# Cross-attention and expert-choice FFN on one core: the attention's counts, reciprocals, score tails and second statistics in other places

## The chip, the cores and the metric

The kernel runs on one core of one Trainium2 chip. Its engines are TensorE (PE, with its weight loads PEld), VectorE (DVE), ScalarE (ACT), GpSimd (POOL) and SyncE (SP), which here only starts transfers. The metric is the device time in microseconds (us) of one execution; the profile's span lies inside it.

## The reference

```python
x = x + xattn(layernorm(x), ctx)          # x: (2, 2048, 512); ctx: (2, 77, 384); 8 heads of 64
    # softmax(q k^T / 8) v, then @ Wo + bo
x = x + ffn(layernorm(x))                 # 8 experts, hidden 2048
    # probs = softmax(x @ gate_w.T); each expert takes its top k tokens of a sequence
    # out[token] += gate * (gelu(x_token @ w1) @ w2)
```

All of it is in float32. The kernel builds float32 products from fp32r parts: high by high, high by low, low by high (hence three matmuls wherever one product stands).

## The kernel before

**Stages.** Setup folds Wq and Wk into A (one matrix per batch, 8 folds) and Wv and Wo into B (10 folds), so that attention is scores = XN A, softmax, out = P B. The gate's eight columns ride along in both (SC, OC). The gate columns of B come from 24 small matmuls (`pe_gate_fold`, L1036) and go back into `wo_sb` and `bo_row` on DVE (L990 to L994) before the B folds. Then comes attention: 16 blocks of two tiles of 128 tokens (NBLK = 16, TPB = 2), in steps i = -1 to 16, in a pipeline over several blocks. Then come the experts: the chosen rows are gathered and run through up, Gelu and down.

**One attention step i.** Every engine has its own fixed order (`step` in `pe_attention`, `act_attention`, `dve_attention`, `pool_attention`, `sp_attention`); semaphores join them. PE: transposes of the probabilities of block i-1 (L1095; the last 104 columns of each tile are the tails), scores of block i in two tiles of two halves (L1056 to L1058, `three`), output product of block i-1 tile 0, transposes of the normalised block i+1 (`pe_xT`, L1032), output product tile 1. ACT: high parts of the transposed probabilities (`pTh`, tails first, L847, L848), eight exps per tile with the row sum (`exp`, L839), normalising of block i-2 into XN2 (L819), gate exps of block i-2 (L811), high part of the transposed block (`xTh`, L826), normalising of block i+2. DVE: `dve_x1` (x + attention and the gate logits, L911, L913), low parts (`pTl` L945, L949, `xTl` L919), the score maximum as a minimum of the negated scores (L931), statistics by bn_stats and bn_aggr of the residual X1 (block i-2) and of x (block i+2) (L875, L880), reciprocals of the row sums (L925), gate (L894 to L900). POOL: small [128, 2] steps that make the reciprocal deviation (`pool_rstd2` L752, `pool_rstd1` L732), gate logit repair, and scaling of the probabilities by the reciprocals (L803). The transposes wait for that scaling.

**Counts.** Which 512 tokens an expert takes is found by a search of 15 rounds (`dve_round` L523, `pe_round` L553): DVE narrows the threshold by the last totals, makes three candidates, compares and counts per partition (L549); PE sums over partitions with a matrix of ones (L555). For batch 0 these rounds run in steps 9 to 14, up to three per step (`round_at`, slots 0, 1, 2). Slot 2 of a step is counted by PE at the start of the next one, slot 0 after the transposes, slot 1 before the last score half. Masks and places follow in steps 14 and 15 (`dve_masks`, `dve_chosen`, `dve_places`, `dve_rows`), then the rows are looked up by a one-hot product (L646, L654), and POOL gathers them (L786) at step 16.

## Time and profile before

| | |
|---|---|
| median of 3 runs | 1773.19 us (1773.03 to 1773.25) |
| profiled execution | 1772.58 us, its span 1770.9 us |
| PE busy | 1702.3 us (96%), 8702 matmuls |
| DVE, ACT, POOL busy | 1099.1, 798.9, 346.5 us |
| granted PE clock, mean | 0.979 |

How to read the rows further down. In windows: stretch, its length, busy time and instructions (x) of PE, PEld, DVE, ACT, POOL, then the granted clock of TensorE (1.00 is 2.4 GHz, 0.50 is 1.2 GHz), the DMA share and GB/s. In waits: who waited for whom, us in total, times, longest. In the timeline: start, duration, engine, line, operation, output and input, count, and in brackets the idle time ahead of it and what ended it. In groups: busy us and mean ns, then idle time. A step begins with its first transpose (L1095): 87.0 (step 2), 103.1, 120.5, 137.8, 155.4, 172.9, 190.3, 207.9, 228.5 (step 10), 251.8, 276.2, 299.5, 321.6, 340.8, 361.2.

### The profile page before, as it was taken

How to read it: one execution, taken by the hardware profiler on the slowest of the kernel's cores; microseconds unless marked ns; L12 is line 12 of the kernel's file. 1: busy time of each engine (PE TensorE's matmuls, PEld its weight loads, DVE VectorE, ACT ScalarE, POOL GpSimd, SP SyncE). 2: the span in 40 equal slices, each digit the busy share in tenths (PEclk: the TensorE clock that was granted, in tenths of full speed). 3: DMA queues.
4: the chain of work that ended last, by engine and by line, in shares of the span. 5: the costliest groups of instructions: out<-in, count | busy, mean ns of one | idle time of the engine just before them, and what ended most of it. 6: DMA issues, size and time to landing. Idle time of an engine off the chain costs nothing.

```text
span 1770.9 us, 23364 instructions
## 1 busy us (share of the span) xinstructions
PE 1702.3 (96%) x8702; PEld 1448.2 (82%) x8702; DVE 1099.1 (62%) x2020; ACT 798.9 (45%) x1852; POOL 346.5 (20%) x457
## 2 busy tenths in 40 slices
PE   7999978879999999999999999999999999999997
PEld 7898978867888888888888888888888888888886
DVE  5355566667686665775575557556766675575563
ACT  4466644452332333444454445444544454454441
POOL 2133322230010302240034005100700160022002
PEclk9899988989999999999999999999999999999999
DMA  3133323323243525251134114411511261133003
GB/s 125 58 110 117 122 96 135 127 84 122 93 119 119 167 95 143 95 143 48 48 73 117 48 48 90 124 49 48 133 58 49 71 143 48 48 72 71 24 1 48
DMA packets 76660, 156.36 MB, mean 88 GB/s; under 512 B 4453, under 2 KB 5633, under 8 KB 76553
## 3 DMA queue, kind: packets, MB, share of 16 engines
q1 hardware_dynamic: 62217, 121.38, 20.0%
q0 software_dynamic: 14336, 33.56, 9.7%
q8 instruction: 67, 1.10, 0.3%
q14 instruction: 40, 0.33, 0.1%
HBM read 121.37 MB, written 33.55 MB: 87 GB/s over the span
## 4 chain that ended last, share of the span: by engine, by line
PE 85%; DVE 6%; issue 3%; POOL 3%; ACT 2%; DMA 0%; POOLq 0%; DVEq 0%; ACTq 0%
PE ps L1868 10%; PE ps L1870 10%; PE ps L1869 10%; PE ps L1846 9%; PE ps L1848 9%; PE ps L1847 9%; PE ps L1761 3%; PE ps L1762 3%; PE ps L1763 3%; PE ps L1748 3%; PE ps L1749 3%; PE ps L1750 3%; PE ps L1056 2%; DVE st L875 2%; PE ps L1057 2%
## 5 line engine op out<-in xcount | busy, mean ns | idle before, releaser
L1868 PE MATMUL ps<-v2h,hhS 128*128 128x512 f32 x768 | 300.5, 391 | 0.0
L1870 PE MATMUL ps<-v2h,hlS 128*128 128x512 f32 x768 | 298.9, 389 | 0.0
L1869 PE MATMUL ps<-v2l,hhS 128*128 128x512 f32 x768 | 298.9, 389 | 0.0
L1846 PE MATMUL ps<-Th,Wh 128*128 128x512 f32 x672 | 261.4, 389 | 0.0
L1847 PE MATMUL ps<-Tl,Wh 128*128 128x512 f32 x672 | 261.4, 389 | 0.0
L1848 PE MATMUL ps<-Th,Wl 128*128 128x512 f32 x672 | 261.4, 389 | 0.0
L1301 POOL DMA_INDIRECT out_dram<-YS,tok_idx x48 | 80.5, 1678 | 805.5 <-DVE YS L1655 797.2
L1421 ACT ACTIVATE v2h<-w_raw 128x512 fp32r<-128x512 f32 x96 | 57.7, 625 | 308.6 <-PE ps L1870 308.6
L1655 DVE SCALAR_TENSOR_TENSOR YS<-ps,tok_gate,YS 128x512 f32<-128x512 f32 x144 | 106.6, 749 | 132.1 <-PE ps L1870 132.1
L1870 PEld LDWEIGHTS ps<-v2h,hlS 128*128 128x128 f32 x768 | 144.1, 188 | 30.2
L1869 PEld LDWEIGHTS ps<-v2l,hhS 128*128 128x128 f32 x768 | 144.2, 188 | 29.4
L1868 PEld LDWEIGHTS ps<-v2h,hhS 128*128 128x128 f32 x768 | 144.2, 188 | 29.0
L1638 DVE TENSOR_TENSOR hlS<-hfS,hhS 128x512 fp32r<-128x512 f32 x192 | 128.0, 687 | 45.0 <-ACT hfS L1440 45.0
L1439 ACT ACTIVATE hhS<-hfS 128x512 fp32r<-128x512 f32 x144 | 91.1, 632 | 129.8 <-DVE hfS L1627 61.6
L1848 PEld LDWEIGHTS ps<-Th,Wl 128*128 128x128 f32 x672 | 126.1, 188 | 26.3
L1847 PEld LDWEIGHTS ps<-Tl,Wh 128*128 128x128 f32 x672 | 126.1, 188 | 26.3
L1846 PEld LDWEIGHTS ps<-Th,Wh 128*128 128x128 f32 x672 | 126.1, 188 | 26.0
L1748 PE MATMUL ps<-eTh,w1h 128*128 128x512 f32 x256 | 102.5, 401 | 5.5 <-issue 5.5
L1761 PE MATMUL ps<-w2h,hh 128*128 128x512 f32 x256 | 103.1, 403 | 0.0
L1762 PE MATMUL ps<-w2l,hh 128*128 128x512 f32 x256 | 100.8, 394 | 0.0
L1763 PE MATMUL ps<-w2h,hl 128*128 128x512 f32 x256 | 100.7, 393 | 0.0
L1749 PE MATMUL ps<-eTl,w1h 128*128 128x512 f32 x256 | 100.7, 393 | 0.0
(236 smaller groups left out, 3517.1 us busy)
## 6 DMA issues: line engine op xcount, KB each, us to landing
w_raw<-in_L_ffn_w_dram SPq DMA_DIRECT2D x80, 1024.0 KB, 5.5
XB<-in_x_dram SPq DMA_DIRECT2D x16, 512.0 KB, 4.2
XR<-in_x_dram SPq DMA_DIRECT2D x16, 512.0 KB, 6.0
out_dram<-X SPq DMA_DIRECT2D x16, 512.0 KB, 5.0
xn_rows<-XN SPq DMA_DIRECT2D x16, 512.0 KB, 5.5
w_raw<-in_L_xattn_Wq_dram SPq DMA_DIRECT2D x1, 1024.0 KB, 8.2
wo_sb<-in_L_xattn_Wo_dram SPq DMA_DIRECT2D x2, 512.0 KB, 10.0
w_raw<-in_L_xattn_Wk_dram SPq DMA_DIRECT2D x1, 768.0 KB, 4.8
```

The source lines that it names most:

```text
L1638: nc.vector.tensor_tensor(hlS[:, b, f], hfS[:, b, f], hhS[:, b, f].bitcast(F32), ALU.subtract).then_inc(s_hid, 1)
L1748: nc.tensor.matmul(ps[:, 4 + n % 2, :], wh, th, start=(k == 0), stop=False)
L1749: nc.tensor.matmul(ps[:, 4 + n % 2, :], wh, tl, start=False, stop=False)
L1761: nc.tensor.matmul(ps[:, c, :], th, wh, start=(f == 0), stop=False)
L1762: nc.tensor.matmul(ps[:, c, :], th, wl, start=False, stop=False)
L1763: last = nc.tensor.matmul(ps[:, c, :], tl, wh, start=False, stop=(f == KF - 1))
L1846: nc.tensor.matmul(ps[:, bank, :], wh, th, start=(idx in OPENS and k == 0), stop=False, **go_on)
L1847: nc.tensor.matmul(ps[:, bank, :], wh, tl, start=False, stop=False, **go_on)
L1848: last = nc.tensor.matmul(ps[:, bank, :], wl, th, start=False, stop=(k == 1), **go_on)
L1868: nc.tensor.matmul(ps[:, bank, :], th, wh, start=(t == 0), stop=False)
L1869: nc.tensor.matmul(ps[:, bank, :], th, wl, start=False, stop=False)
L1870: last = nc.tensor.matmul(ps[:, bank, :], tl, wh, start=False, stop=(t == GF - 1))
```

## The change

- x1 is a scalar_tensor_tensor that also sums the row (`sum2`). POOL makes minus the mean from it (`pool_mean2`), ACT squares the centred row with a sum (`act_squares`, into XN2 as a scratch), POOL goes on with that variance. bn_stats and bn_aggr of X1 are gone.
- ACT: the squares stand ahead of the exps, the gate exps between the two tiles' exps, the two tiles of XN2's normalising on both sides of xTh. After step 16 the squares of the last block stand ahead of the experts.
- DVE: gate scores and gate move ahead, the second reciprocal ahead of x1 and xTl; the statistics of x are taken in two halves around the maxima; round 0 after the tails, round 1 after the first maximum, round 2 before the second reciprocal.
- PE: both tiles' scaling is waited for once, the tails are transposed first with a semaphore of their own; round 0 is counted between the score tiles, round 1 after the scores, round 2 in the middle of output tile 1. POOL scales tile 0 ahead of `pool_rstd1`.
- Step 0: the first scores start ahead of Wo's transposes, the small gate matmuls are put between the matmuls of the last score half, B folds use three pairs of banks.
- Step 15: row numbers, values and one-hot stand later on DVE.

```diff
+        def fold_bank(n):
+            return (6, 2, 4)[(n - NA) % 3]
...
-            if n >= 4:
-                pe.wait_ge(e_lo, n - 3 if kind == "A" else max(n - 1, NA))
+            if kind == "A" and n >= 4:
+                pe.wait_ge(e_lo, n - 3)
+            if kind == "B" and n >= NA + 3:
+                pe.wait_ge(e_lo, n - 2)
...
-            return BANK[1] if b == 1 else 0 if k % SLOTS == 0 else 3
+            return BANK[0] if b == 0 and k % SLOTS == 0 else BANK[1]
...
+        def pool_mean2(pool, n):
+
+            pool.wait_ge(v_x1, (n + 1) * TPB)
+            if not isinstance(n, int) or n > 0:
+                pool.wait_ge(a_sq2, n)
+            pool.tensor_tensor(nm2[:], sum2[:], minus_over_d[:], ALU.mult).then_inc(g_nm2, 1)
+
         def pool_rstd2(pool, n, u, i):
 
-            pool.wait_ge(v_mv2, n + 1)
+            pool.wait_ge(a_sq2, n + 1)
+            pool.tensor_tensor(ve2[:], ssq2[:], over_d[:], ALU.mult).then_inc(g_var2, 1)
+            pool.wait_ge(g_var2, n + 1)
+            pool.tensor_tensor(ve2[:], ve2[:], eps_c[:], ALU.add).then_inc(g_ve2, 1)
+            pool.wait_ge(g_ve2, n + 1)
             if not isinstance(n, int) or n > 0:
                 pool.wait_ge(a_gexp, n)
-            pool.tensor_tensor(nb2[:], mv2[:, :, 0], minus_c[:], ALU.mult)
-            pool.tensor_tensor(ve2[:], mv2[:, :, 1], eps_c[:], ALU.add).then_inc(g_ve2, 1)
-            pool.wait_ge(g_ve2, n + 1)
+                pool.wait_ge(a_xn2, n)
             pool.tensor_tensor(rs2[:], ve2[:], pow_c[:], ALU.pow).then_inc(g_rs2, 1)
+            pool.wait_ge(g_ring, i + 2)
+            pool.wait_ge(g_nm2, n + 1)
+            pool.tensor_tensor(gdm[:], ring[u][:, 4, TPB:2 * TPB], nm2[:], ALU.add).then_inc(g_dm, 1)
             pool.wait_ge(g_rs2, n + 1)
-            pool.tensor_tensor(nb2[:], nb2[:], rs2[:], ALU.mult).then_inc(g_nb2, 1)
-            pool.wait_ge(g_ring, i + 2)
-            pool.tensor_tensor(gdm[:], ring[u][:, 4, TPB:2 * TPB], mv2[:, :, 0], ALU.subtract).then_inc(g_dm, 1)
+            pool.tensor_tensor(nb2[:], nm2[:], rs2[:], ALU.mult).then_inc(g_nb2, 1)
...
                     pool_rstd2(pool, i - 2, u, i)
+
+                def scale(t):
+                    pool.wait_ge(v_rec, 2 * i + t + 1)
+                    over = srec[:, t * H:(t + 1) * H].unsqueeze(2).broadcast_to([P, H, J])
+                    pool.tensor_tensor(PR[:, t], PR[:, t], over, ALU.mult).then_inc(g_prob, 1)
+
+                if has(i):
+                    scale(0)
                 if has(i + 2):
                     pool_rstd1(pool, i + 2, u)
                 if has(i):
-                    for t in range(TPB):
-                        pool.wait_ge(v_rec, 2 * i + t + 1)
-                        over = srec[:, t * H:(t + 1) * H].unsqueeze(2).broadcast_to([P, H, J])
-                        pool.tensor_tensor(PR[:, t], PR[:, t], over, ALU.mult).then_inc(g_prob, 1)
+                    scale(1)
             steps(pool, step)
...
+        def act_squares(act, n, u):
+
+            act.wait_ge(g_nm2, n + 1)
+            for t in range(TPB):
+                last = nc.scalar.activation(XN2[:, u, t, :], X1[:, u, t, :], ACT.Square, bias=nm2[:, t:t + 1],
+                                            accum_out=ssq2[:, t:t + 1])
+            last.then_inc(a_sq2, 1)
...
                 if has(i - 1):
+                    act.wait_ge(p_tails, i)
+                    nc.scalar.activation(pTh[0:TAIL, :, NCH - 1, :], tails, ACT.Copy).then_inc(a_tails, 1)
                     act.wait_ge(p_pT, i)
-                    nc.scalar.activation(pTh[0:TAIL, :, NCH - 1, :], tails, ACT.Copy).then_inc(a_tails, 1)
...
+                if has(i - 2):
+                    if not isinstance(i, int) or i >= 4:
+                        act.wait_ge(d_xn2[u], 16 * half - 16)
+                    act_squares(act, i - 2, u)
...
                 if has(i):
                     exp(i, 0, u)
+                if has(i - 2):
+                    act_gate_exp(act, i - 2)
+                if has(i):
                     exp(i, 1, u)
                 if has(i - 2):
-                    if not isinstance(i, int) or i >= 4:
-                        act.wait_ge(d_xn2[u], 16 * half - 16)
-                    act_normalise(act, X1[:, u], rs2, nb2, XN2[:, u], g_nb2, a_xn2, i - 2)
-                    act_gate_exp(act, i - 2)
+                    act_normalise(act, X1[:, u], rs2, nb2, XN2[:, u], g_nb2, a_xn2, i - 2, (0,))
                 if transposed(i, has):
                     act_xTh(act, i + 1)
+                if has(i - 2):
+                    act_normalise(act, X1[:, u], rs2, nb2, XN2[:, u], g_nb2, a_xn2, i - 2, (1,))
...
+            act.wait_ge(d_xn2[(NBLK - 1) % 2], 16 * (NBLK // 2 - 1))
+            act_squares(act, NBLK - 1, (NBLK - 1) % 2)
...
-            nc.vector.tensor_tensor(X1[:, u, t].rearrange("p (h d) -> p h d", h=2), out_halves(t),
-                                    XR[:, u, t].rearrange("p (h d) -> p h d", h=2), ALU.add).then_inc(v_x1, 1)
+            nc.vector.scalar_tensor_tensor(out=X1[:, u, t].rearrange("p (h d) -> p h d", h=2), in0=out_halves(t),
+                                           scalar=1.0, in1=XR[:, u, t].rearrange("p (h d) -> p h d", h=2),
+                                           op0=ALU.mult, op1=ALU.add, accum_out=sum2[:, t:t + 1]).then_inc(v_x1, 1)
...
             def step(i, u, half, has):
...
                 if has(i - 2):
                     dve_x1(dve, i - 2, 1, u, None, None)
-                if round_at(i, 0) is not None:
-                    dve_round(dve, 0, round_at(i, 0))
                 if has(i - 1):
                     dve.wait_ge(a_tails, i)
...
+                if round_at(i, 0) is not None:
+                    dve_round(dve, 0, round_at(i, 0))
+                if has(i - 1):
                     dve.wait_ge(a_pTh, i)
...
-                if round_at(i, 1) is not None:
-                    dve_round(dve, 0, round_at(i, 1))
                 if at(i, CHOICE + 1):
                     dve_places(dve, 0, 1)
-                    dve_rows(dve, 0)
-                    dve_vals(0, 0, 1)
-                    dve_one_hot(0)
-                if has(i):
-                    maximum(i, 0)
-                if has(i - 2):
-                    if not isinstance(i, int) or i > 2:
-                        dve.wait_ge(g_dm, i - 2)
-                    dve.wait_ge(v_x1, 2 * i - 2)
-                    stats(X1[:, u], st2, v_st2)
                 if has(i + 2):
                     dve.wait_ge(d_x[u], 16 * half + 32)
                     if has(i + 1):
                         dve.wait_ge(g_sd, i + 2)
-                    if has(i - 2):
-                        dve.wait_ge(v_st2, i - 1)
-                    stats(XB[:, u], st1, v_st1)
-                elif has(i - 2):
-                    dve.wait_ge(v_st2, i - 1)
+                    nc.vector.bn_stats(st1[:, 0, :], XB[:, u, 0, :])
+                if has(i):
+                    maximum(i, 0)
+                if at(i, 0):
+                    dve.wait_ge(p_woT, 2)
+                    for c in range(2, KD):
+                        nc.vector.tensor_copy(woT[:, c, :], ps[:, 4 + c, :]).then_inc(e_woT, 1)
+                if round_at(i, 1) is not None:
+                    dve_round(dve, 0, round_at(i, 1))
                 if has(i - 2):
-                    aggregate(st2, mv2, v_mv2)
-                if has(i + 2):
-                    dve.wait_ge(v_st1, i + 3)
-                if at(i, CHOICE):
-                    dve.wait_ge(p_s, 2 * i + 2)
-                    dve_masks(dve, 0)
+                    dve_gate_scores(dve, i - 2)
+                if at(i, 0):
+                    dve.wait_ge(p_boT, 1)
+                    nc.vector.tensor_copy(boT[:], ps[:, 5, 64:64 + KD]).then_inc(e_boT, 1)
                 if has(i):
                     maximum(i, 1)
                 if has(i + 2):
+                    nc.vector.bn_stats(st1[:, 1, :], XB[:, u, 1, :]).then_inc(v_st1, 1)
+                    dve.wait_ge(v_st1, i + 3)
+                if has(i):
+                    reciprocal(i, 0)
+                if has(i + 2):
                     aggregate(st1, mv1, v_mv1)
+                if at(i, CHOICE + 1):
+                    dve_rows(dve, 0)
+                if has(i - 2):
+                    dve_gate(dve, i - 2)
+                if round_at(i, 2) is not None:
+                    dve_round(dve, 0, round_at(i, 2))
+                if at(i, CHOICE):
+                    dve_masks(dve, 0)
+                if has(i):
+                    reciprocal(i, 1)
+                if has(i - 1):
+                    dve_x1(dve, i - 1, 0, 1 - u, 16 * half + 16 * u,
+                           16 * half - 16 + 16 * u if not isinstance(i, int) or i >= 3 else None)
                 if at(i, 0):
                     dve.wait_ge(p_wog, 1)
...
-                if has(i - 2):
-                    dve_gate_scores(dve, i - 2)
-                if has(i):
-                    reciprocal(i, 0)
-                if has(i - 1):
-                    dve_x1(dve, i - 1, 0, 1 - u, 16 * half + 16 * u,
-                           16 * half - 16 + 16 * u if not isinstance(i, int) or i >= 3 else None)
                 if transposed(i, has):
                     dve_xTl(dve, i + 1)
-                if has(i - 2):
-                    dve_gate(dve, i - 2)
-                if has(i):
-                    reciprocal(i, 1)
...
-                if round_at(i, 2) is not None:
-                    dve_round(dve, 0, round_at(i, 2))
...
                 if at(i, CHOICE + 1):
+                    dve_vals(0, 0, 1)
+                    dve_one_hot(0)
                     dve_found(dve, 0, BANK[0])
...
-
+            def three(psum, pairs, terms=None):
...
+                def others():
+                    if terms:
+                        for _ in range(2):
+                            next(terms, None)
+                    nc.tensor.matmul(psum, wh, mh, start=(k == 0), stop=False)
+                    others()
+                    nc.tensor.matmul(psum, wh, ml, start=False, stop=False)
+                    others()
+                    last = nc.tensor.matmul(psum, wl, mh, start=False, stop=(k == n - 1))
+                    if k < n - 1:
+                        others()
 
...
+            def first_scores():
+
+                pe.wait_ge(e_gwl, B)
+                pe.wait_ge(d_wo, 32)
+                pe.wait_ge(d_bo, 32)
+                for t in range(TPB):
+                    for part in range(2):
+                        if t == 0:
+                            pe.wait_ge(e_lo, 5)
+                        elif part == 0:
+                            pe.wait_ge(e_lo, NA)
+                            for c in range(KD):
+                                for k in range(KD):
...
+                            pe.wait_ge(e_woT, KD)
+                        terms = pe_gate_terms() if t and part else None
+                        scores(0, t, part, terms)
...
             def step(i, u, half, has):
                 if has(i):
                     pe.wait_ge(v_xTl, i + 1)
-                if round_at(i - 1, 2) is not None:
-                    pe_round(pe, 0, round_at(i - 1, 2))
                 if has(i - 1):
                     if at(i, 1):
-                        pe.wait_ge(e_lo, len(folds))
-                    pe.wait_ge(g_prob, 2 * i - 1)
+                        pe.wait_ge(e_lo, len(folds) - 1)
+                    pe.wait_ge(g_prob, 2 * i)
                     if has(i - 2):
                         pe.wait_ge(v_lg, 2 * i - 3)
                     flat = PR[:].rearrange("p t h j -> p (t h j)")
                     for t in range(TPB):
-                        if t:
-                            pe.wait_ge(g_prob, 2 * i)
-                        for c, (c0, n) in enumerate(CH):
-                            dst = tails[:, t, :] if c == NCH - 1 else ps[:, 4 + t, c0:c0 + P]
-                            last = nc.tensor.transpose(dst, flat[:, t * HJ + c0:t * HJ + c0 + n], ident[:])
+                        c0, n = CH[-1]
+                        last = nc.tensor.transpose(tails[:, t, :], flat[:, t * HJ + c0:t * HJ + c0 + n], ident[:])
+                    last.then_inc(p_tails, 1)
+                    for t in range(TPB):
+                        for c, (c0, n) in enumerate(CH[:-1]):
+                            last = nc.tensor.transpose(ps[:, 4 + t, c0:c0 + P],
+                                                       flat[:, t * HJ + c0:t * HJ + c0 + n], ident[:])
                     last.then_inc(p_pT, 1)
-                if round_at(i, 0) is not None:
-                    pe_round(pe, 0, round_at(i, 0))
                 if at(i, 0):
...
+                    first_scores()
+                elif has(i):
                     for t in range(TPB):
                         for part in range(2):
                             if has(i - 1) and (t, part) == (0, 1):
                                 pe.wait_ge(v_tails, i)
+                            if round_at(i, 0) is not None and (t, part) == (1, 0):
+                                pe.wait_ge(v_lg, 2 * i - 2)
+                                pe_round(pe, 0, round_at(i, 0))
                             if at(i, CHOICE + 1) and (t, part) == (1, 0):
                                 pe_before(pe, 0, 1)
                             if at(i, CHOICE + 1) and (t, part) == (1, 1):
                                 pe.wait_ge(s_placed, 2)
-                            if round_at(i, 1) is not None and (t, part) == (1, 1):
-                                pe_round(pe, 0, round_at(i, 1))
...
+                            scores(i, t, part)
+                if round_at(i, 1) is not None:
+                    pe_round(pe, 0, round_at(i, 1))
                 if at(i, 0):
...
+                    pe_gate_bias(pe)
                 if has(i - 1):
+                    if at(i, 1):
+                        pe.wait_ge(e_lo, len(folds))
                     pe.wait_ge(v_pTl, i)
                     out_tile(i, 0)
...
+                    pe.wait_ge(a_exp, 2)
                     for n in range(NA, len(folds)):
                         pe_fold(pe, n)
                 if has(i - 1):
                     if has(i - 2):
                         pe.wait_ge(v_lg, 2 * i - 2)
-                    out_tile(i, 1)
-                    if at(i, CHOICE):
-                        pe.wait_ge(a_exp, 2 * i + 2)
-                        pe_before(pe, 0, 0)
+
+                    def between():
+                        if round_at(i, 2) is not None:
+                            pe.wait_ge(a_exp, 2 * i + 2)
+                            pe_round(pe, 0, round_at(i, 2))
+                        if at(i, CHOICE):
+                            pe.wait_ge(a_exp, 2 * i + 2)
+                            pe_before(pe, 0, 0)
+
+                    out_tile(i, 1, between)
```

## Rows read from the trace of the kernel before

**Rows 1.** Windows by stage: quiet step, steps 3-9, 10-14, hand-over, experts.

```profile
87.00:103.10 16.10, 16.10 (x128) 16.10 (x126) 9.34 (x22) 11.03 (x45) 4.89 (x16) 1.00 0.21 66
103.10:225.40 122.30, 114.56 (x884) 112.29 (x882) 67.47 (x169) 77.19 (x315) 41.15 (x112) 1.00 0.35 121
225.40:340.80 115.40, 94.88 (x650) 91.85 (x649) 76.88 (x221) 53.71 (x223) 28.08 (x74) 0.88 0.37 128
340.80:385.40 44.60, 30.94 (x222) 29.49 (x222) 28.88 (x80) 18.43 (x61) 14.99 (x31) 0.82 0.28 95
385.40:1770.90 1385.50, 1370.36 (x6356) 1130.94 (x6356) 877.74 (x1454) 602.24 (x1102) 239.41 (x172) 0.99 0.29 82
```

**Rows 2.** Waits of PE, 0 to 420 us.

```profile
PE ps L555 <- DVE cnt L549: 23.5, 11, 3.7
...
PE ps L1095 <- POOL PR L803: 11.7, 9, 2.8
```

**Rows 3.** Timeline, end of a steady step and start of the next.

```profile
150.87 1.56 ACT L819 ACTIVATE XN<-X,nb,rs 128x512 f32<-128x512 f32 x2
...
152.85 1.06 ACT L826 ACTIVATE xTh<-ps 128x1024 fp32r<-128x1024 f32 x1
...
155.74 0.20 DVE L925 RECIPROCAL srec<-ssum 128x8 f32<-128x8 f32 x1
...
156.02 1.22 POOL L803 TENSOR_TENSOR PR<-PR,srec 128x616 f32<-128x616 f32 x1 [3.48 <-DVE srec L925]
...
157.29 0.77 PE L1095 MATMUL ps<-ident,PR 128*128 128x128 f32 x5 [1.13 <-POOL PR L803]
```

**Rows 4.** Timeline, the first counts.

```profile
226.16 0.93 DVE L541 TENSOR_TENSOR cand<-kept,bits 128x24 uint32<-128x24 uint32 x1
...
228.42 0.17 PE L555 MATMUL ps<-cnt,ones_bf 128*128 128x24 bf16 x1 [2.89 <-DVE cnt L549]
...
229.29 0.18 DVE L541 TENSOR_TENSOR cand<-kept,bits 128x24 uint32<-128x24 uint32 x1
...
230.10 0.55 DVE L549 TENSOR_REDUCE cnt<-hit 128x24 bf16<-128x384 bf16 x1
```

**Rows 5.** Windows after small matmuls and after the count waits.

```profile
45.80:55.40 9.60, 9.60 (x24) 6.31 (x24) 2.30 (x7) 1.63 (x2) 2.61 (x3) 0.50 0.00 0
...
229.90:236.60 6.70, 5.89 (x23) 5.89 (x24) 3.92 (x11) 1.26 (x2) 0.00 (x0) 0.50 0.47 172
```

**Rows 6.** Groups of DVE and ACT, steps 3 to 9.

```profile
L875 DVE BATCH_NORM_STATS2 st<-X 128x6 f32<-128x512 f32 x14 | 8.9, 680 | 0.0
...
L911 DVE TENSOR_TENSOR X<-ps,XR 128x512 f32<-128x512 f32 x14 | 9.4, 672 | 5.7 <-PE ps L1058 5.4 <-issue 0.3
...
L949 DVE TENSOR_TENSOR pTl<-ps,pTh 128x1024 fp32r<-128x1024 f32 x7 | 8.6, 1225 | 3.4 <-ACT pTh L848 3.4
...
L931 DVE TENSOR_REDUCE nmax<-ps 128x8 f32<-128x616 f32 x14 | 11.2, 800 | 6.2 <-PE ps L1058 6.2
...
L819 ACT ACTIVATE XN<-X,nb,rs 128x512 f32<-128x512 f32 x14 | 10.9, 852 | 0.0
...
L839 ACT ACTIVATION_READ_ACCUMULATOR PR<-ps,nmax 128x1 f32 x112 | 25.0, 223 | 0.0
```

**Rows 7.** Timeline, one-hot, gathers and hand-over to the experts.

```profile
352.36 2.29 DVE L646 TENSOR_TENSOR hot<-row,col_iota 128x2048 bf16<-128x2048 f32 x1
...
365.11 1.22 POOL L786 DMA_INDIRECT XB<-xn_rows,tok_idx  x1 [0.40 <-DMA xn_rows<-XN]
...
370.13 0.24 POOL L750 TENSOR_TENSOR ring<-ring,one_c 128x16 f32<-128x16 f32 x1
...
378.21 0.63 ACT L1346 ACTIVATE w1h<-w_raw 128x512 fp32r<-128x512 f32 x1 [4.30 <-PE ps L1058]
...
383.40 1.28 ACT L1362 ACT_TABLE_LOAD   x1
...
385.46 0.76 PE L1748 MATMUL ps<-eTh,w1h 128*128 128x512 f32 x1 [5.53 <-issue]
```

116 lines of the change are left out of this document (54 added, 62 removed).

## The prediction

> **What bounds the kernel now.** I first read the windows by stage [rows 1]: attention runs to 385.4 us, the experts take the other 1385.5 us. TensorE (PE) is busy in the experts and in the quiet attention step 2 (16.10 of 16.10 us). In steps 3 to 9 it is busy 114.56 of 122.3 us, in steps 10 to 14 94.88 of 115.4 us at a mean granted clock of 0.88, in steps 15 and 16 and the hand-over 30.94 of 44.6 us. The change touches the experts in one place only, so at most what attention loses is on offer. The list of waits [rows 2] names the losers: PE waits 23.5 us in eleven pieces for the counts (L549), 11.7 us in nine pieces for the scaled probabilities (L803). One such piece in a steady step [rows 3]: ScalarE (ACT) is done with both exps at 150.87, but the second reciprocal comes at 155.74 (on VectorE, DVE, it stands behind x1, the residual split and the gate, which waits for ACT's gate exps, which stand behind the normalising of XN2). GpSimd (POOL) then scales 1.22 us and PE starts the second half of its transposes at 157.29, after 1.13 us idle. The first step with counts [rows 4]: PE asks for count 0 right after the output product, DVE has only begun it, PE gets it at 228.42 after 2.89 us; the next round needs another chain of 1.8 us (0.4 for narrowing, then 229.29 to 230.65). These two waits cost more than they last: after the pair the granted clock is 0.50, the 1.2 GHz level, for 6.7 us [rows 5], where 6.7 us of work takes about 3.3 us at 2.4 GHz. Steady steps with one idle piece of 1.1 us stay at 1.00 [rows 1].
>
> **Steady steps 3 to 9.** Set T = 0 at the first transpose of a step; PE's own work is 16.1 us [rows 1]: transposes to 1.1, scores to 8.0 (about 1.72 per product group), output tile 0 to 11.6, xT to 12.4, output tile 1 to 16.1. New order:
> - Exps end at 150.87 - 137.8 (this step's first transpose) less 1.4 of its stall, about T = 11.7. Two gate exps now stand ahead of the second group, 0.6 us (they fit between the normalising's last start-up, 150.87 + 1.4, and 152.85 [rows 3]): 12.3. The reciprocal follows, now ahead of x1 and the split (0.2), then scaling 1.22: 13.8. PE wants it at 16.1, both tiles ahead of the first transpose. Cover 2.3 us; the wait goes.
> - The squares: two ACT passes of 512 with an accumulator read. Nearest rows: Identity of the same width 0.852, the read 0.223 [rows 6]; with their overlap 1.7 per step, bounds 1.6 and 2.2. They start when POOL has the mean (x1 of tile 1 ends near T = 1.1; mean at 1.4) and the pTh copy is over, 2.2, and end at 3.9. ACT had waited there until 5.6 for the score maximum, so they are free with 1.7 us of cover; without it, ACT delays the exps by what is missing.
> - Behind them POOL's chain (two scalings now, power 0.7, four small ones) takes 2.5: the gate logits are there at 6.5, the maximum subtraction on DVE at about 7, before ACT wants it at 8.3. What is queued behind ACT's new wait for it are the second exps, for whom POOL and PE wait; cover 1.3.
> - DVE loses two statistics passes of 0.680 on X1 and an aggregate (-1.6 per step), and x1 becomes a scalar_tensor_tensor with a sum: 0.672 now [rows 6]; no row shows the new form, I take +0.06, bounds 0 and +0.3 (an accumulator read of its own, 0.223 on ACT). Of these the lower is nearer: both are one pass over the same operands. Both x1 are off the path (cover 1 us).
> - After the exps: XN2 tile 0 to 13.1, xTh to 14.2, xTl on DVE to 15.4: the residual is 0.7 us early for the next scores.
> - SP: XN2's second tile is normalised after xTh, 1.6 us later than now, and with it go the store of XN2 and the XR load queued behind it. That load waits for the x1 at T = 1.1 of the next step anyway and is read 11 us after it, the store's buffer a whole step later; I cost it at nothing. Without that cover it would be those 1.6 us per step.
> So a step takes 16.1. 7 x 16.1 = 112.7 against 122.3: **-9.6** (bounds -8 and -10).
>
> **Steps 10 to 14 (counts).** Round 0 moves behind the tail residual on DVE, PE takes it between the two score tiles (T = 4.5); round 1 is taken after the scores (T = 8.0), round 2 in the middle of output tile 1 (T = 14.3). DVE's queue: x1 with logits from 0.35 to 1.2, tails to 1.65, round 0 to 3.45 (1 us early), residual 1.22 to 4.7, one statistic 0.68 to 5.35, maximum 0.80 to 6.15 [rows 6], round 1 to 7.95. PE wants that at 8.0: here nothing is left, I take 0.3 us of stall. Round 2 runs from 10.8 to 12.7, 1.6 early; then reciprocal, x1, split to 15.8 against 16.4. With three count matmuls of about 0.12 a step is 16.1 + 0.4 + 0.3 = 16.8; 5 x 16.8 = 84.0 against 115.4: **-31.4** (bounds -33 with no stall, -27 with 1.2 us). About 13 of this are the clock, since no idle piece is left that is longer than those the steady steps survive at 1.00.
> A queue the change moves work past: POOL scales tile 0 at T = 10.0 to 11.2, under round 2. DVE's candidate op needed 0.93 us at 226.16, while POOL scaled, and 0.18 at 229.29, alone [rows 4]. That is up to 1 us late in round 2, of which 0.6 is covered: part of the upper bound. The Trainium skill (GPSIMD Engine Reference, Specifications) says the same against this change: GpSimd shares its SBUF interfaces with VectorE and contends with ops of two SBUF inputs. By that rule the hit op would be slowed too, some 0.5 us a step, 2.5 us in all; the trace shows no hit op under a scaling.
>
> **Hand-over, steps 15 and 16.** 44.6 us before from step 15's first transpose to the first up matmul (340.80 to 385.46 [rows 1, 7]). New: the one-hot (2.29, [rows 7]) is queued behind x1 instead of ahead of the maxima; DVE ends it at T = 17.6 while PE has finished step 15 at 15.5: 2.1 idle. Lookup and indices to 19.0. POOL issues four gathers, 5.0 (365.11 to 370.13 [rows 7]): 24.1. Only then the mean of block 14 (24.6), squares (26.3), POOL chain (28.8), gate maximum, gate exps, gate: 30.9; the last two x1 to 32.6, though PE is done near 31 (its clock will be halved, as before). Mean of block 15, squares: 34.7. They stand ahead of the experts' first weights on ACT, which began at 378.21 before, as soon as PE was done. From there DVE's four weight halves and four token residuals, 6.0: up at 40.7. **-3.9** (bounds 0 and -6).
>
> **Setup.** The 24 small gate matmuls go between the last score matmuls: the same work, but score tile 1 of step 0 is complete only when nearly all of them are through (about 4 us later than now, as they take 0.2 us each), its exps end later by as much, and the folded gate columns on DVE now stand behind their reciprocal. PE reaches the first scores 3.3 us earlier, for it no longer waits for the last A folds, but loses that and 1.4 us more in these waits before the B folds. With three bank pairs the waits at their end shrink by 1.4. Whether the clock still halves is open: it was 0.50 for 9.6 us, 4.8 us lost [rows 5]; since an idle stretch of near 3 us now follows the thin work, I expect it does, for 8 us instead. These are sizes from my walk, not rows. **-0.6** (bounds +1.5; -5 if the clock stays).
>
> **Sum.** 9.6 + 31.4 + 3.9 + 0.6 = 45.5. The profiled execution took 1772.58 (span 1770.9); the median of the runs is 0.6 above it, 1773.19. 1772.58 - 45.5 + 0.6 = **1727.7**. The experts stay at 1385.5.
>
> **Rivals.**
> - *Count steps stay held up.* DVE has about 14 us of work in a step of 16.8, all in order, and round 1 has no cover. If it comes 2 us or more late, PE stalls and the clock halves again, as in [rows 5]: 1.5 more stall and 3.3 more of clock in each of five steps, about +17 (half of them: +9): 1737 to 1745. For it: the thin margin; against it: no piece in my walk above 0.3. 17%.
> - *A function-table load for each change between Square and Exp.* The trace has one load at the start and the next, 1.28 us, only with Gelu at 383.40 [rows 7]; Copy, Identity and Exp share a table, Square is not shown. Two loads per step put ACT at 11.03 + 1.7 + 2.6 = 15.3 busy and the exps 0.9 late, more than the residual's 0.7: about +0.8 in 14 steps: 1739. 5%. The Trainium skill (ScalarE: Activation LUTs, Table sets: the hidden batching unit) says tables come in sets with cheap functions as filler in all of them, without naming square; by that the load doesn't come. Its 2.66 us for a switch would make 5.3 per step and about 1775; the row has 1.28.
> - *Slower.* PE now takes no transpose until both tiles are scaled, and POOL's second scaling stands behind the statistics of block i+2, which hang on the squares' chain. If the second scaling ended at T = 18 or later (4.2 us behind my walk), PE would idle 2 us at each step's start with nothing issued, and the clock would halve each time: 2 + 3.5 in 14 steps, +77: 1805. From +3.3 per step on the kernel is slower than now. It takes squares or POOL steps two to three times their rows. 3%.
> - *It doesn't do what it says:* the stalls move but sum to the same, 1773. 1%.
>
> **Chances.** Forecast 74%, its own range 1720 to 1735. Range 1719 to 1742: lower end with the clock kept in the setup and the full hand-over, upper end into the first rival. A measurement of this kernel tells about 0.2%, 3.5 us, from no change: faster 0.95, same 0.02, slower 0.03.
>
> **What would show it.** No PE wait on L803's scaling in steps 3 to 14; steps of 16.1 and 16.8; granted clock 1.00 from step 3 to step 14; ACT's wait for the maximum shortened by the squares' 1.7; second reciprocal right behind the exps; a PE wait of about 2 for the one-hot; ACT's first weight copy after the last squares. I am wrong if PE waits at the step's start, if ACT idles in front of the gate exps, if Square brings loads, or if the clock falls in a count step.

## The result and the profile after

The changed kernel takes 1726.76 us (median of four runs, 1725.1 to 1729.0) against 1773.11 for the kernel before on the same chip: ratio 0.9745, 95% interval 0.9727 to 0.9762. Its profiled execution took 1729.0 with a span of 1727.3. The prediction, 1727.7, holds in its total. Part by part it holds less well, and the experiments say which reasons were right. The profiled execution is the slowest of the four, so the parts read from it below add up to less (43.6) than the medians give (46.4).

Windows by stage of the changed kernel: step 2, steps 3 to 9, steps 10 to 14, hand-over, experts. Columns as in [rows 1].

```profile
89.51:105.65 16.14, 16.14 (x129) 16.14 (x127) 9.21 (x22) 12.65 (x49) 6.02 (x17) 1.00 0.22 66
105.65:218.75 113.10, 113.10 (x885) 113.05 (x884) 65.66 (x165) 88.53 (x343) 42.31 (x119) 1.00 0.38 131
218.75:301.06 82.31, 82.31 (x649) 81.11 (x648) 69.16 (x205) 61.82 (x243) 28.84 (x79) 1.00 0.50 178
301.06:341.91 40.85, 29.93 (x224) 29.05 (x223) 23.52 (x65) 22.17 (x73) 14.32 (x32) 0.85 0.32 108
341.91:1727.30 1385.39, 1370.42 (x6356) 1130.95 (x6356) 877.71 (x1454) 602.31 (x1103) 239.30 (x172) 0.99 0.29 82
```

Beside [rows 1]: steps 3 to 9 fell from 122.3 to 113.10 (-9.2), steps 10 to 14 from 115.4 to 82.31 (-33.1), the hand-over from 44.66 to 40.85 (-3.8), the experts stayed, and what lies ahead of step 3 grew from 103.10 to 105.65 (+2.5). The sum is 43.6, the difference of the spans. In steps 3 to 14 PE is busy for the whole stretch. Its waits (all above 1 us that remain between 0 and 420 us) are elsewhere:

```profile
PE ps L1824 <- issue: 6.4, 1, 6.4
PE ps L275 <- DMA ctx_sb<-in_ctx_dram: 4.0, 1, 4.0
PE ps L565 <- DVE cnt L559: 3.7, 1, 3.7
PE ps L1099 <- DVE pTl L992: 2.4, 1, 2.4
PE ps L664 <- DVE hot L656: 2.1, 1, 2.1
PE ps L301 <- DVE xTl L965: 1.9, 1, 1.9
PE ps L288 <- DMA w_raw<-in_L_xattn_Wk_dram: 1.6, 1, 1.6
PE ps L330 <- DVE bo_row L1042: 1.6, 1, 1.6
```

Against [rows 2], the 23.5 us for counts are down to one piece of 3.7 (the experts' first count, there before too), the 11.7 for scaled probabilities are gone. The timeline at the end of a steady step answers [rows 3]:

```profile
149.72 0.20 DVE L971 RECIPROCAL srec<-ssum 128x8 f32<-128x8 f32 x1 [0.46 <-ACT PR L874]
149.93 0.69 DVE L956 SCALAR_TENSOR_TENSOR X<-ps,XR 128x512 f32<-128x512 f32 x1
150.66 1.21 POOL L822 TENSOR_TENSOR PR<-PR,srec 128x616 f32<-128x616 f32 x1
151.70 1.23 DVE L965 TENSOR_TENSOR xTl<-ps,xTh 128x1024 fp32r<-128x1024 f32 x1 [1.00 <-ACT xTh L861]
154.07 0.38 PE L1183 MATMUL ps<-ident,PR 128*104 128x128 f32 x2
```

The reciprocal comes right behind the exps, scaling ends at 151.87, and PE takes it 2.2 us later without idling. In a count step (the answer to [rows 4]) DVE is ahead of PE each time:

```profile
254.11 0.55 DVE L559 TENSOR_REDUCE cnt<-hit 128x24 bf16<-128x384 bf16 x1
...
256.16 0.19 PE L565 MATMUL ps<-cnt,ones_bf 128*128 128x24 bf16 x1
...
258.32 0.55 DVE L559 TENSOR_REDUCE cnt<-hit 128x24 bf16<-128x384 bf16 x1
...
259.75 0.19 PE L565 MATMUL ps<-cnt,ones_bf 128*128 128x24 bf16 x1
```

### The profile page after: what moved, and what is told of

It reads as the page before. It is cut to its first block, busy times and chain, and to the rows that moved or that the text cites. A ratio compares the mean times of both kernels' runs of the same rounds, so it can differ in the third digit from the quotient of the medians.

```text
span 1727.3 us, 23439 instructions
## 1 busy us (share of the span) xinstructions
PE 1689.9 (98%) x8702; PEld 1439.9 (83%) x8702; DVE 1084.1 (63%) x1988; ACT 823.4 (48%) x1916; POOL 349.1 (20%) x475
## 3 DMA queue, kind: packets, MB, share of 16 engines
q1 hardware_dynamic: 62217, 121.38, 20.5%
## 4 chain that ended last, share of the span: by engine, by line
PE 96%; DVE 2%; ACT 1%; issue 0%; DMA 0%; POOL 0%; SPq 0%; DVEq 0%; ACTq 0%
PE ps L1945 10%; PE ps L1944 10%; PE ps L1946 10%; PE ps L1923 9%; PE ps L1922 9%; PE ps L1924 9%; PE ps L1099 4%; PE ps L1103 4%; PE ps L1101 4%; PE ps L1837 4%; PE ps L1838 3%; PE ps L1839 3%; PE ps L1824 3%; PE ps L1825 3%; PE ps L1826 3%; PE ps L1881 1%
## 5 line engine op out<-in xcount | busy, mean ns | idle before, releaser
L1439 ACT ACTIVATE hf<-ps 128x512 f32<-128x512 f32 x64 | 38.3, 598 | 132.0 <-PE ps L1826 132.0
```

## The experiments

Each is timed against the kernel before on the same chip, whose medians were 1773.07 (b_recip, b_counts, b_filler, a_stats_back), 1771.98 (b_both, b_setup_new, a_split_vals, a_squares_late), 1770.72 (a_gate_early, a_tokens_first, a_old_setup) and 1771.44 (a_gate_early_old_setup). Between runs of different groups compare the ratios, not the times. Theory: one move, the early reciprocal, gives the steady steps; the counts' places with it give the count steps, and of that more than ten us are TensorE's clock; squares on ACT matter only where DVE is full; the setup gives nothing. Rival: the lighter DVE queue (the squares) carries the gain, and the moves only shift the waits.

**b_recip.** The kernel before with one line moved.

```diff
+                if has(i):
+                    reciprocal(i, 1)
                 if has(i - 1):
                     dve_x1(dve, i - 1, 0, 1 - u, ...
...
-                if has(i):
-                    reciprocal(i, 1)
```

> The kernel before with one line moved: DVE takes the second reciprocal of a step ahead of x1(i-1,0), the split and the gate; squares, counts, tails and PE's order stay as before. Theory (the wait of steps 3 to 9 is the reciprocal's place on DVE alone): scaling of tile 1 starts at 151.1 instead of 156.02, the PE wait on L803 goes, steps 3 to 9 take 16.1 to 16.2 us each, -8 to -9.5 us there; steps 10 to 14 hardly move (-0 to -2), because the same stretch is covered by the count wait; total 1762 to 1765. Rival (the squares' room on DVE and the new ACT order carry it): the steady steps stay above 16.8 and the total above 1768.

1754.08 us, ratio 0.9894 (0.9878 to 0.9911). Windows of steps 3 to 9 and 10 to 14:

```profile
106.37:219.40 113.03, 113.02 (x884) 112.48 (x882) 67.99 (x169) 77.08 (x315) 40.75 (x112) 1.00 0.38 131
221.88:326.02 104.14, 92.17 (x648) 89.11 (x647) 70.71 (x208) 53.67 (x223) 27.85 (x74) 0.90 0.39 140
```

The first is the changed kernel's 113.1: this line is the whole steady gain, with statistics, tails and ACT's order untouched. The total is 8 us below the theory's range, for the count steps gained too, where I had expected 0 to 2: by the same marks (first transposes of step 10 to those of step 15) 104.14 against 112.26. The wait at their start shrank from 2.9 to 2.0, four times, and the clock was low for 20.4 instead of 27.3 us.

**b_counts.** The kernel before with the counts' places alone.

```diff
+                            if round_at(i, 0) is not None and (t, part) == (1, 0):
+                                pe.wait_ge(v_lg, 2 * i - 2)
+                                pe_round(pe, 0, round_at(i, 0))
...
+                if round_at(i, 1) is not None:
+                    pe_round(pe, 0, round_at(i, 1))
```

> The kernel before with only the places of the counts changed on DVE and PE as in the changed kernel (round 0 behind the tail residual and between the score tiles, round 1 behind the first maximum and after the scores, round 2 ahead of x1 and in the middle of output tile 1; count 0 stays at the step's start). Reciprocal, statistics and the tails stay. Theory: steps 3 to 9 stay at 17.5 us; steps 10 to 14 fall from 23.1 to 17.9 each (16.1 of work, 0.4 for the counts, up to 1.4 of the old reciprocal wait), clock 1.00 from step 11 on, -24 to -27 us; total 1747 to 1749. Rival 1 (DVE has no room without the squares, round 1 comes late and the clock halves again): -8 to -15, total 1758 to 1765. Rival 2 (the waits only move): total above 1768.

1758.83 us, ratio 0.992 (0.9903 to 0.9937): it gained 10 us less than the theory said, and lies inside rival 1's band but not by its mechanism. Round 1 is on time. PE's waits at the start of one step:

```profile
249.28 0.77 PE L1100 MATMUL ps<-ident,PR 128*128 128x128 f32 x5 [1.01 <-DVE xTl L919]
...
251.15 1.12 PE L1100 MATMUL ps<-ident,PR 128*128 128x128 f32 x4 [1.10 <-POOL PR L803]
```

Round 2 now stands ahead of x1 and the reciprocal, so x's residual comes late as well, and the old scaling wait is uncovered. Two pieces of 1.0 and 1.1 us, 0.8 us apart, and the granted clock falls to 0.50 for 3.4 us behind each such pair, four times (a fifth low stretch follows the count wait of 3.0 us ahead of step 10); the steady steps of the kernel before, with one piece of 0.9 to 1.3 us, stay at 1.00. The count steps take 20.0 on average, three of them 20.5, not 17.9.

**b_both.** The two edits together, the reciprocal behind round 2.

> The kernel before with the two edits that were run alone before put together: the counts' new places and the second reciprocal ahead of x1 (behind round 2). Statistics, tails, gate, ACT's order and the setup stay. Alone they gave 18.4 and 13.0 us of span against the profile of before, 31.4 together if they only add. Theory (each idle piece of PE alone is short; what costs is two of them within a step, since then the clock halves, so the edits need each other): steps 2 to 8 at 16.14, steps 10 to 14 at 16.5 to 17.7 with the granted clock at 1.00, total 1731 to 1737. What is left to the changed kernel (+4 to +10) is the residual of x, which DVE with its first and second statistics ends up to 1.2 us after PE wants it. Rival 1 (the gains only add): 1740 to 1743, with halved clock in the count steps. Rival 2 (statistics and tails play no part): within 2 us of the changed kernel's 1726.8.

1736.88 us, ratio 0.9809 (0.9794 to 0.9824). Windows of steps 3 to 9 and 10 to 14, and the wait that is left in the count steps:

```profile
102.97:215.80 112.83, 112.83 (x883) 112.39 (x882) 67.92 (x168) 76.95 (x315) 40.76 (x112) 1.00 0.38 131
218.41:308.47 90.06, 85.40 (x649) 82.84 (x648) 69.77 (x208) 53.65 (x223) 28.96 (x74) 0.98 0.46 162
```

```profile
PE ps L1100 <- DVE xTl L919: 4.0, 4, 1.0
PE ps L555 <- DVE cnt L549: 2.8, 2, 2.2
```

The theory's time, at its upper end, but its count steps were to take 16.5 to 17.7 us at a clock of 1.00, and take 18.0 on average at 0.98; rival 2 is out by 10 us. That the edits need each other isn't shown: steps 10 to 14 fell by 22.2, the two alone give 8.1 and 12.1, together 20.2, so the gains nearly add. What the other parts of the change are worth together is shown: 10 us lie between this kernel and the changed one. The second maximum stands behind four statistics passes here, so exps, xTh and xTl are 1.0 late, four times; the single idle pieces of 1.0 us that this leaves don't lower the clock.

**a_stats_back.** The changed kernel with the second statistics on DVE again, no squares.

```diff
+                if has(i - 2):
+                    ...
+                    stats(X1[:, u], st2, v_st2)
+                    dve.wait_ge(v_st2, i - 1)
                 if has(i - 1):
                     dve.wait_ge(a_pTh, i)
                     ...
+                if has(i - 2):
+                    aggregate(st2, mv2, v_mv2)
```

> The changed kernel with the second statistics as before (x1 a plain sum, two BATCH_NORM_STATS2 and the aggregate on DVE, placed behind the tail residual and round 0, ahead of the big residual, while DVE waits for the pTh copy; no squares on ACT). Theory (the squares give the steady steps nothing that they need, they pay only where DVE is full): steps 3 to 9 stay at 16.1 to 16.2; in steps 10 to 14 round 1 comes 1.6 us later against a cover of 0.9, +0.5 to +1.2 each, +3 to +6 in all (more if the clock halves); hand-over within 0.5; total 1730 to 1734. Rival (the squares carry the steady gain): steady steps at 16.8 or more, total above 1736.

1730.16 us, ratio 0.976 (0.9743 to 0.9776). Steps 3 to 9, and one count step:

```profile
106.30:219.40 113.10, 113.10 (x886) 113.05 (x884) 74.70 (x179) 78.71 (x315) 40.69 (x112) 1.00 0.38 131
...
253.50:270.51 17.01, 16.62 (x131) 16.22 (x130) 14.91 (x42) 11.05 (x45) 5.82 (x16) 1.00 0.50 175
```

Steady steps the same, count steps 17.0 instead of 16.45, of which 0.4 is a wait for round 1, four times. So the squares give 2.3 us there, less than the theory's 3 to 6. They take it back in the hand-over, 38.56 us here against 40.85 (the theory had no more than 0.5), and the spans are 1726.8 and 1727.3. But the changed kernel's profile is its slowest execution and this one's is not: by the medians this kernel is 3.4 us slower, with intervals that overlap. So as a part of the change the squares are worth between 0 and 3 us; the runs don't say more. And this kernel, without squares, is some 7 to 9 us below b_both (by medians and by ratios): what b_both lacks are for the most part the other places (statistics, tails, gate, ACT's order), and no run takes those apart.

**b_filler.** The kernel before with matmuls that nobody reads in PE's waits.

```diff
+                filler(20, 0)
...
+                filler(6, 3)
                 if round_at(i, 0) is not None:
```

> The kernel before with matmuls of 312 columns that nobody reads in PE's waits of steps 10 to 14: 20 at the step's start (2.9 us) and 6 ahead of round 0 (0.9 us). No wait becomes shorter; PE only stays busy in it. Theory (about 13 us of the count steps are the halved clock): the granted clock of steps 10 to 14 is 1.00 instead of 0.88, score matmuls behind the wait take 0.30 instead of 0.46 us, and the stretch falls from 115.4 to 102 to 106 us (13 back, less up to 1 us per step where the filler is longer than the wait); total 1760 to 1765. Rival (the clock costs nothing, since the count is late anyway and sets the step): the clock rises but the stretch stays at 113 to 118, total 1771 to 1776. Third: the clock doesn't rise, since it isn't the idle piece that lowers it.

1762.6 us, ratio 0.994 (0.9924 to 0.9957). Steps 10 to 14:

```profile
230.40:332.89 102.49, 99.61 (x758) 96.77 (x757) 73.87 (x207) 53.72 (x223) 26.69 (x72) 1.00 0.40 141
```

The counts come no earlier within a step, yet 112.26 became 102.49: 9.8 us are the clock alone. In the kernel before it was low for 27.3 us in these steps; PE was busy for 23.7 of them and so lost 11.8 us of work. Why 2 us of that don't come back is not shown (in one step the filler left a wait of 1.6 us).

**b_setup_new and a_old_setup.** The new setup in the kernel before, and the old setup in a_tokens_first (below). Both swap `first_scores`, `fold_bank`, the gate terms and DVE's copies of step 0 as a whole.

> The kernel before with only the new setup and step 0: gate matmuls between those of the last score half, three bank pairs for the B folds, the first scores from five A folds on, DVE's copies in the new order. From the end of the A folds (27.7 to 27.8 us in each profile) to step 1's first transposes the old order took 43.2, 44.7, 45.1 and 46.4 us in four profiles, the new one 45.6 and 46.2 in two. Theory (the new order is worth nothing or costs about 1 us, since the thin matmuls now spread over a longer stretch at the halved clock): 45 to 47 us there, 1.5 to 3.5 us less clock, total 1772 to 1776. Rival (my -0.6 of the prediction, the profile of after having only met a late fall of the clock): 42.5 to 44.5 us, total 1770 to 1772.5.

> a_tokens_first with the setup and step 0 of the kernel before (gate matmuls in a block behind the scores, two bank pairs, all A folds ahead of the scores, DVE's copies as before). In this kernel no step behind the setup idles, so the total shows the setup alone. Theory from the profiles (start of step 1 at 70.8 to 74.2 in five with the old order, 72.9 to 75.4 in five with the new; the clock is low for 10.2 us in four of the old ones and for 17.1 in three of the new): the old setup is faster, total 1 to 2.5 us below a_tokens_first. Rival (my -0.6, and b_setup_new, which was 2.8 us faster than before by its runs): total 0.5 to 3 us above.

b_setup_new, with the new order: 1768.68 us, ratio 0.9984 (0.9975 to 0.9993), a little faster than its pair and below both ranges expected. a_old_setup, with the old order: 1718.49, ratio 0.9703 (0.9689 to 0.9716), against 1722.01 and 0.9719 (0.9704 to 0.9734) for its pair, 3.5 us lower too, though the intervals overlap. Both can't be the setup's own doing. I put all fourteen profiles side by side, by the time of step 1's first transposes, with the sum of the clock's low stretches up to there, both in us (old: the kernel before, b_recip, b_counts, b_filler, b_both, a_old_setup, a_gate_early_old_setup; new: the changed kernel, a_stats_back, b_setup_new, a_split_vals, a_squares_late, a_gate_early, a_tokens_first):

```
old order  70.89/10.2  74.16/17.1  72.42/10.2  72.86/10.2  70.76/10.2  74.21/13.6  70.98/10.2   mean 72.3/11.7
new order  73.35/17.1  74.00/17.1  72.89/13.7  74.20/17.1  75.36/20.5  74.44/17.1  74.09/17.1   mean 74.1/17.1
```

Windows of the changed kernel and of a_gate_early_old_setup in the low stretch (to set beside [rows 5]):

```profile
43.00:60.00 17.00, 15.11 (x52) 10.88 (x52) 4.16 (x13) 4.84 (x20) 4.03 (x9) 0.50 0.00 1
```

```profile
44.80:54.80 10.00, 10.00 (x37) 7.04 (x37) 2.56 (x9) 1.63 (x2) 4.02 (x9) 0.50 0.00 0
```

The new order costs 1.7 us up to step 1 in the mean, with profiles of either order between 72.9 and 74.2, and the low stretch is 5.4 us longer. That b_setup_new was faster all the same lies behind it, where it changes nothing: in its profile steps 10 to 14 take 108.48 instead of 112.26, with the clock low for 23.9 instead of 27.3 us. So in a kernel that idles in these steps an edit ahead of them went with other falls of the clock; in steps 1 to 14 of the changed kernel there are none to move. Why the time fell in ten of eleven runs is open. My theory missed b_setup_new's time, as its rival did, and had a_old_setup's direction right and its size (1 to 2.5) too small.

**a_split_vals, a_squares_late, a_gate_early, a_tokens_first, a_gate_early_old_setup.** What the waits list has left, on top of the changed kernel.

> The changed kernel with DVE's work for batch 0's gate values (3.4 us in the experts' slot 0) cut: there only expert 1's (about 0.7), the others two by two in slots 4, 6 and 8. PE waits 3.73 us for the first count of batch 1 at 361.77, and the clock is 0.74 in the ten us behind. Theory: the DVE queue in front of that count is 2.7 us shorter, the wait falls to about 1.0, the clock stays up: -2.7 and -2 to -2.6 of clock, total 1721.5 to 1723. Rival (the rest comes back as late counts in slots 4 to 8, where DVE has 1.9 us of round and 2.5 of weights and residuals in a slot of 5.1): PE waits on L559 there, total 1725 to 1729.

> The changed kernel with block 15's squares behind ACT's first weight halves, token chunks and third weights instead of ahead of them. Theory (in the hand-over the squares hold ACT from 334.84 to 336.27, so the first weight copy, DVE's residuals and the first up matmul come as much later): first weight copy right behind PE's last output matmul, PE's idle piece ahead of the first up matmul 5.5 instead of 6.4 us, total 1725.5 to 1726.5, -0.8 to -1.4. Rival (DVE's four weight and four token residuals set the end): no change, or a later gate of block 15 that shows as a longer wait for the first count.

> The changed kernel with block 15's squares behind the token chunks (as in a_squares_late), its gate chain ahead of the first Gelu (gate exps on ACT behind the third weights, gate and expert 1's values on DVE ahead of the first hidden residual), the other values in slots 4, 6 and 8 (as in a_split_vals). Splitting the values alone left the wait for the first count at 3.7 us: DVE then waited 1.54 us for ACT's weights, which stand behind the gate exps and two table loads of 1.28. Theory: with the gate exps under the exp table, ACT's two extra loads (L837 and the one behind it) and the gate exps, 3.4 us, leave the chain; the first count comes 3 to 3.7 us earlier, PE's wait for it falls to 0 to 0.7, the clock falls once less (-1.7): total against a_squares_late's 1725.5: -4 to -5.4, so 1720 to 1721.5. Rival (the late one-hot of 2.29 and DVE's weights set the count): wait stays above 2, total 1723 to 1726.

> a_gate_early with the four token chunks of expert 0 ahead of the second weights on ACT and DVE. Theory: the first up matmul needs one pair of weight residuals less, 1.0 to 1.4 us: PE's idle piece ahead of it 2.6 to 3.0 instead of 4.0 us, total 1 to 1.4 below a_gate_early. Rival: the second up product waits for its weights instead, no change.

> a_gate_early with the setup and step 0 of the kernel before, as in a_old_setup, without the token chunks' new place. Theory (the old setup is worth what it gave a_tokens_first, 1722.0 to 1718.5, since the clock is low for 10 to 14 us instead of 17; the token chunks gave nothing, for PE waited 1.5 us for the first count where it had waited 0.3): 0.9690 to 0.9710 of before, 1717 to 1719.5 us, and the setup's low stretches 10 to 14 us in sum. Rival (that difference was the draw of the clock's falls; b_setup_new had it the other way round): 1720 to 1723, no different from a_gate_early.

a_split_vals: 1727.38, ratio 0.9746 (0.9733 to 0.976), no change. The values were not what the count waited for; DVE idles behind them:

```profile
352.45 0.69 DVE L1588 TENSOR_TENSOR w1l<-w_raw,w1h 128x512 fp32r<-128x512 f32 x1 [1.54 <-ACT w1h L1423]
...
362.50 0.20 PE L565 MATMUL ps<-cnt,ones_bf 128*128 128x24 bf16 x1 [3.71 <-DVE cnt L559]
```

ACT stands there behind block 15's gate exps and their table loads. a_squares_late: 1725.46, ratio 0.9738 (0.9725 to 0.9751); its hand-over took 36.93 instead of 40.85, more than expected, since the idle piece went from 6.4 to 4.0 and the low clock became 3.4 us shorter; half of it is hidden in its profile by its setup, the slowest of all (75.36), and its total, by the ratios 1.2 us below the changed kernel's, isn't clear of noise. a_gate_early puts both together and the gate exps ahead of the first Gelu:

```diff
+                if n == 0:
+                    act.wait_ge(d_xn2[(NBLK - 1) % 2], 16 * (NBLK // 2 - 1))
+                    act_squares(act, NBLK - 1, (NBLK - 1) % 2)
                 if n + 2 < NPL:
                     weights(n + 2)
+                if n == 0:
+                    act_gate_exp(act, NBLK - 1)
```

1720.59, ratio 0.9719 (0.9705 to 0.9733), as the theory had it: the first count is nearly there,

```profile
356.36 0.19 PE L565 MATMUL ps<-cnt,ones_bf 128*128 128x24 bf16 x1 [0.33 <-DVE cnt L559]
```

and the experts take 1378.9 instead of 1385.4. a_tokens_first (1722.01, 0.9719, interval 0.9704 to 0.9734) was to be 1 to 1.4 us faster and isn't: it won 1.2 us ahead of the first up matmul and lost them to the count, whose wait rose from 0.3 to 1.5. a_gate_early_old_setup: 1716.18, ratio 0.9693 (0.968 to 0.9706), 4.4 us below a_gate_early and the fastest kernel here, about 10 us below the changed one. 3.5 us of its profile's 5.6 are the setup; 0.7 come from steps 1 to 8, at 16.05 instead of 16.14 each, which I can't explain.

## Why the prediction was right, and where it wasn't

**The total.** Its fit is in part luck. Against the profiled execution the sum of 45.5 is 1.9 too high: the setup's term was 3.1 us too favourable, that of the count steps 1.7 too unfavourable. That execution lies 2.2 us above the median of the four, and this covers the rest.

**Steady steps** (-9.6 predicted, -9.2 measured): the mechanism and the size hold. At T (time from the step's first transpose, here 137.93) the second reciprocal came at 11.8 (walk: 12.3), the scaled tile at 13.9 (13.8), squares ran from 2.2 to 3.7 (2.2 to 3.9), the gate logits were there at 5.8 (6.5), the split ended at 15.0 (15.4). The prices, from the groups of steps 3 to 9 (beside [rows 6]):

```profile
L854 ACT ACTIVATE XN<-X,nm 128x512 f32<-128x512 f32 x14 | 9.9, 713 | 0.0
...
L956 DVE SCALAR_TENSOR_TENSOR X<-ps,XR 128x512 f32<-128x512 f32 x14 | 9.6, 687 | 9.5 <-PE ps L1103 9.4
...
L956 DVE DVE_READ_ACCUMULATOR X<-ps,XR 128x1 f32 x14 | 1.2, 83 | 0.0
```

x1 with its sum costs 0.015 more and a read of 0.083, near the +0.06 taken, not the 0.3. The text gave the gain to the new order and the lighter DVE as one; b_recip shows it was the reciprocal's place alone. The squares, to which most of that part's working went, bring nothing here.

**Count steps** (-31.4 predicted, -33.1 measured): the term "0.3 of stall at round 1" was mis-sized; it is 0. Round 1 is ready at T = 7.2, not 7.95, and PE takes it at 8.1. I had added whole durations on DVE (1.22, 0.68, 0.80), but each operation starts about 0.1 ahead of the end of the one before: in the rows of step 11 they follow at 1.13, 0.65 and 0.71. These three make 0.2 of the 0.7; the residual had started 0.5 ahead of the walk already (T = 2.94, not 3.45), since x1 began 0.15 sooner and the operations behind it overlap in the same way. "About 13 of this are the clock" was near: 11.8 us of work were lost to it, and b_filler shows that 9.8 can be had without curing the waits. The parts are not what I listed either: b_both gets 22.2 of steps 10 to 14, the lighter or better ordered DVE the next 8 us.

**POOL beside DVE.** No hit op lay under a scaling, so the 0.5 us per step that I had worked out never came up. The gate's two multiplications did lie there, and took 1.28 us together where they take 0.37 alone:

```profile
261.66 1.22 POOL L822 TENSOR_TENSOR PR<-PR,srec 128x616 f32<-128x616 f32 x1 [4.21 <-DVE srec L971]
261.78 1.28 DVE L945 TENSOR_SCALAR probs<-gexp,grec 128x8 f32<-128x8 f32 x2
```

That is why round 2 was ready at T = 13.1 instead of 12.7; its cover of 1.4 took it. The Trainium skill (GPSIMD Engine Reference, Specifications) names contention for DVE operations with two SBUF inputs or in a 2-port performance mode. The multiplication has one SBUF tensor and a per-partition scalar; the trace agrees that it contends, and doesn't show by which of the two conditions.

**Hand-over** (-3.9 predicted, -3.8 measured; the gathers take 5.0 as in [rows 7]): the walk holds from piece to piece: one-hot at 17.5 (17.6), gathers at 24.1 (24.1), squares of block 14 at 26.1 (26.3), the last x1 at 33.4 (32.6), first up at 40.85 (40.7). The walk had no row for the 2.4 us in which PE waits for pTl at 323.56; the squares of block 15, which it placed rightly, cost 2.4 us of idle (a_squares_late has 4.0 where the changed kernel has 6.4) and some clock.

**Setup** (-0.6 predicted, +2.5 in the profile): the sign was wrong. The step that failed is "I expect it does, for 8 us instead": the low stretch became longer, 17.1 instead of 10.2 us, in five of seven profiles 17.1. I gave the clock the fall of before and shortened it by the idle piece; in fact PE does thin work at 0.50 from 43 us on, waits 1.64 us for the bias row in it, and the stretch runs on through the B folds. Over seven profiles each the loss is 1.7 us, in kernels without idle steps behind it 3.5 and 4.4 us by the medians. All lie beyond the term's bound of +1.5.

**Rivals.** The held-up count steps and the idle at the step's start did not come: PE has no wait in steps 3 to 14. The first one's price was added up wrongly: 1.5 and 3.3 us in each of five steps are 24, not 17, so about 1752 instead of 1745. Square brought no table load, the trace has none between 0.81 and 341.43 us; the rule of the Trainium skill (ScalarE: Activation LUTs, Table sets: the hidden batching unit), that cheap functions sit in every set, doesn't name square, and the trace agrees with it for square too.

## What to carry to other kernels

A small instruction that a far engine waits for (a reciprocal of 0.2 us) goes ahead of everything in its queue that only the next step needs: here one moved line was 19 of the 46 us. Undo each part alone before crediting it: here the two moves carry the change, the cheaper statistics give little or nothing, and the reordered setup loses. Read what stands behind the engine that is named in a wait (a_split_vals removed 2.4 us of DVE work and nothing came of it, for ACT was the one that was late).

## What was not expected of the hardware

- The granted clock fell to 0.50 with PE idle for only 1.0 and 1.1 us, 0.8 us apart, in four steps of b_counts, while single pieces of 0.9 to 1.3 us left it at 1.00 in the kernel before. This is no fixed rule: in step 13 of b_recip pieces of 2.0 and 0.9 us, 1.4 us apart, left it at 1.00, and in b_filler two of 0.8 and 1.1 us, 0.8 us apart (332.1 to 334.8 us), did too, where the same two in the kernel before (340.0 to 342.7 us) were followed by a fall.
- Under a POOL operation on two SBUF tensors some small DVE operations without any PSUM operand stretch until POOL is done: the gate's two multiplications (0.37 to 1.28 us), the candidates of a round (0.18 to 1.03 in the kernel before), a 128x128 step of the places (1.32). Others do not: in the kernel before a TENSOR_REDUCE of the round (L521) keeps its 0.19 us under the scaling, in b_both a RECIPROCAL of 128x8 does; nor do x1 at 0.64 and the split at 1.22 us, which read PSUM.
- A steady step took 16.05 us in the profile of a_gate_early_old_setup and 16.14 in those of the changed kernel and its other six variants.
